# Squares of a unit taken one unit ahead, GpSimd's roots in another rhythm, block two's raw rows loaded between the contexts' loads, gates stored in scan order

## The chip, the core and the metric

The kernel runs on one core of a Trainium2 chip. The metric is the time of one execution on the device in microseconds (us), taken as the median of three runs. The engines are TensorE (PE, its weight loads PEld), VectorE (DVE), ScalarE (ACT), GpSimd (POOL) and SyncE (SP), which here only issues transfers. ACTq, POOLq and SPq are the engines' instruction queues, where transfers are issued.

## What is computed

A decoder block on 16 sequences of 256 tokens, width 256, in float32. The change touches only the first of its layers, and the preparation of the second:

```python
xn = _rmsnorm(x, norm1_w)                       # x*rsqrt(mean(x*x)+eps)*w
xc = _causal_depthwise_conv(xn, conv_w, conv_b) # 4 taps over time, then silu
q = _l2norm((xc @ wq)...); k = _l2norm((xc @ wk)...); v = (xc @ wv)...
beta = sigmoid(xc @ wb); alpha = sigmoid(xc @ wa + 4)
for each of 256 tokens, 16 sequences x 16 heads, S of 16 x 16:
    S = a * S;  pred = S^T k
    S = S + k (b * (v - pred))^T
    o = S^T q
h = x + o @ wo; then a gated MLP, layernorm
cross-attention on 120 context rows per sequence, layernorm
routed feed-forward (8 experts, top 1), layernorm
```

## The kernel before

The 256 sequence-heads stand as two halves (`h`) on 128 partitions, and the recurrence over tokens (the scan) runs on VectorE. Time is cut in two blocks of 128 tokens (`jb`), each block in 16 chunks of 8 steps, and each step updates both halves. Block one is scanned in `front_and_scan`, block two in `scan_and_post`, beside the rest of layer one and the attention.

**The front** makes the scan's input. A unit (n = 0 to 15) is 64 tokens of 4 sequences; U = 4 units make one part of 64 tokens for all sequences, and there are four parts. For a unit, SyncE loads rows (`load_rows`), ScalarE sums squares, GpSimd makes 1/rms of two columns (`inverse_rms`, L446), ScalarE (VectorE in part 0) scales the rows to `xn`, TensorE transposes, ScalarE copies to `xT`, TensorE (VectorE in part 0) convolves, ScalarE applies silu, TensorE projects, ScalarE copies q, k, v to `st` and stores them in DRAM, and copies the gates to `bst`, from where they are stored (`store_gates`, L337). A ScalarE step (`step`, L631) works on unit a, on unit b = a-1 and on unit c = a-2, in an order written out by hand. The squares of unit a stand at the head of step a, they use `xn` as scratch, and `xt`, `ss` and `rstd` have two slots. `bst` has one slot: the gate copy of a unit waits until the gate stores of the unit before have landed.

**Before a part is scanned**, `load_raw(part, h)` (L369) loads its k, q, gates and v back in scan order, for one half. This is 3 transfers of 512 KB and 8 of 8 KB on SyncE's queue. `lengths(some, h)` then makes key and query lengths, gate values and scales from them, with squares, sigmoids and square roots on ScalarE and sums and reciprocals on VectorE. For part 0 this stands before the scan. For part 1 VectorE has it woven into chunks 5 and 6 and ScalarE has it after step 2U+4 = 12; for parts 2 and 3 VectorE has it in chunks 14 and 15.

**The read-out** is GpSimd's. After each four steps it makes `outputs(c, z)`, for both halves: one multiply (L246), three folds (L252) and a last add (L254). VectorE keeps 8 states and may not overwrite one before L246 has read it (`S_read`). The same GpSimd makes the roots of units 4 to 15 between read-outs. Units 4 and 5 have theirs ahead of the first read-out and ahead of the two starting increments of `S_read` (L462), units 6 to 12 after the read-outs of chunks 0 to 3, unit 13 to 15 after those of chunks 7 and 8.

**The contexts.** When all convolutions are done, SyncE loads the attention's weights and runs a pipeline over 16 sequences: load `ct(n)`, store `kE(n-2)`, store `vP(n-2)`. `ct` has two slots. TensorE transposes context n and projects keys and values of n-1; ScalarE copies. SyncE has the four `load_raw` of parts 2 and 3 behind the whole pipeline; ScalarE has the lengths of parts 2 and 3 behind the whole pipeline.

Of the kernel before, what the change touches and what calls it, by code (L numbers as in the profile page):

```python
# [7 lines left out]
F32 = mybir.dt.float32  # L8
# [6 lines left out]
P = 128  # L15
# [7 lines left out]
NU = PARTS * U  # L23
R, Q, V, KN, KB = 8, 4, 4, 4, 2
# [7 lines left out]
CTX = 120  # L32
# [231 lines left out]
def front_and_scan(nc, sem, w, k, s, arena):  # L264
# [4 lines left out]
    with ExitStack() as ctx:  # L269
# [6 lines left out]
        xt = sb("xt", [P, 2, 2, D])  # L276
        ss, ms, rstd = (sb(n, [P, 2, 2]) for n in ("ss", "ms", "rstd"))
# [23 lines left out]
        ct, cT = sb("ct", [CTX, 2, D]), sb("cT", [P, 2, G, CTX])  # L301
# [4 lines left out]
        pa = ps("pa", [P, G, 2 * TB])  # L306
        pc = pp[:, 0, :, 0:CTX]
# [5 lines left out]
        x_in, ct_in, kv_out = ([sem(f"f_{n}{i}") for i in range(2)] for n in ("x_in", "ct_in", "kv_out"))  # L313
# [18 lines left out]
        SETUPS = 13  # L332
        TAPS = KC * G
# [3 lines left out]
        def store_gates(eng, n):  # L337

            eng.wait_ge(evac_done, n * 4 + 4)
            for i in range(2):  # L340
                for g in range(G):
                    eng.dma_start(k["gates"][i, n, g].rearrange("a q h t -> h (a q) t"),
                                  bst[32 * i + g * H // G:32 * i + (g + 1) * H // G]).then_inc(gates_out[n >= U], 16)

        @block.sync
        def _(sp):
            def load_rows(n):

                part, u, s = n // U, n % U, n % 2
                if n >= 2:  # L350
                    sp.wait_ge(xn_done, (n - 1) * 2)
# [14 lines left out]
            def load_raw(part, h):  # L366
# [5 lines left out]
                for i, name, dst in ((1, "k", x["k"]), (0, "q", x["q"]), (3, None, None), (2, "v", x["vo"])):  # L372

                    if i == 3:
                        later = part > 0
                        sp.wait_ge(gates_out[later], 64 * (units - U * later))
# [50 lines left out]
        def _(pool):  # L427
# [18 lines left out]
            def inverse_rms(a):  # L446
                if a:
                    n, slot, m = a
                    pool.wait_ge(ss_done, (n + 1) * 2)
                    nc.gpsimd.tensor_tensor(ms[:, slot], ss[:, slot], k["eps"][:, 0], ALU.add).then_inc(rstd_done, 1)  # L450
# [1584 lines left out]
```

## Time and profile before

| | |
|---|---|
| median of 3 runs | 1865.97 us (1862.27 to 1867.58) |
| the profiled execution | 1867.18 us, span 1865.5 us |
| VectorE busy | 1254.0 us, 67% |
| GpSimd busy | 1000.8 us, 54% |
| TensorE busy (matmul) | 1325.9 us, 71% |
| ScalarE busy | 849.6 us, 46% |
| first instruction of the scan | 62.01 us |
| block one's scan ends, block two's starts | about 505 us |

The page gives busy time and share for each engine, then the span in 40 slices, and last the chain that ended last. That chain shows only the end (TensorE in the routed feed-forward, from 1354 us on), so for the stages ahead of it the waits of the engine that is busy there have to be read.

### The profile page before, as it was taken

The page shows a single profiled execution, that of the slowest core. Times are in us where ns is not written, and L with a number is a line of the kernel's source. Part 1 is how long each engine was busy: PE and PEld are TensorE (multiplying, and loading weights), DVE is VectorE, ACT ScalarE, POOL GpSimd, SP SyncE. Part 2 cuts the span into 40 slices and gives each one's busy share as a digit, 9 for nine tenths or more (in the row PEclk, how much of TensorE's full clock was granted, in tenths as well). Part 3 has the DMA queues.
Part 4 walks back from the last instruction along what each step waited for, and adds up shares of the span by engine and source line. Part 5 has one row for each costly group of instructions (what it writes and reads, how often), then busy time and mean ns, then how long its engine had stood idle before and what let it go on. Part 6 is the DMA issues. An engine that isn't in the chain of part 4 may idle for free. (4 is left out here: it accounts for less than half of the span.)

```text
span 1865.5 us, 32852 instructions
## 1 busy us (share of the span) xinstructions
PE 1325.9 (71%) x9000; PEld 1151.7 (62%) x9001; DVE 1254.0 (67%) x3301; ACT 849.6 (46%) x2808; POOL 1000.8 (54%) x1234
## 2 busy tenths in 40 slices
PE   6277106850036676766765899998489999999997
PEld 4265105630025465654654778876389999999997
DVE  3798999999988999999876144454434444443442
ACT  5433213442113665667766488887322322322332
POOL 3367868987669999998866324342111122122121
PEclk9689558885568878878877999998789999999999
DMA  5344001566031010100002111133130410411200
GB/s 139 74 102 111 12 6 42 143 173 95 23 120 38 23 33 18 32 27 27 28 27 84 57 42 52 54 120 120 40 103 21 154 48 22 158 42 45 77 17 7
DMA packets 182719, 119.29 MB, mean 64 GB/s; under 512 B 124849, under 2 KB 163560, under 8 KB 182120
## 3 DMA queue, kind: packets, MB, share of 16 engines
q1 hardware_dynamic: 119848, 90.98, 17.4%
q10 hardware_dynamic: 58864, 18.71, 4.0%
q0 software_dynamic: 3920, 8.60, 1.3%
q8 instruction: 34, 0.56, 0.1%
q14 instruction: 53, 0.43, 0.1%
HBM read 83.44 MB, written 35.74 MB: 64 GB/s over the span
## 5 line engine op out<-in xcount | busy, mean ns | idle before, releaser
L246 POOL TENSOR_TENSOR wt<-wt 128x1024 f32<-128x1024 f32 x128 | 301.5, 2355 | 53.9 <-DVE wt L191 46.9
L252 POOL TENSOR_TENSOR wt<-wt 128x512 f32<-128x512 f32 (+2 forms) x384 | 307.6, 801 | 30.1
L1942 PE MATMUL e_ph<-e_g,e_w 128*128 128x128 f32 x2496 | 285.2, 275 | 0.7 <-ACT e_g L1912 0.7
L1942 PEld LDWEIGHTS e_ph<-e_g,e_w 128*128 128x128 f32 x2496 | 281.9, 192 | 0.9 <-issue 0.9
L191 DVE SCALAR_TENSOR_TENSOR wt<-wt,scan 128x256 f32<-128x256 f32 x512 | 242.0, 473 | 18.0 <-POOL wt L246 13.4
L170 DVE TENSOR_REDUCE wt<-wt 128x16 f32<-128x272 f32 x512 | 219.2, 428 | 0.1
L181 DVE TENSOR_TENSOR scan<-wt,scan 128x256 f32<-128x256 f32 x512 | 215.0, 420 | 0.3
L159 DVE TENSOR_TENSOR wt<-wt,scan 128x256 f32<-128x256 f32 x512 | 210.1, 410 | 0.9 <-PEq L269 0.5
L1420 ACT ACTIVATE wt<-p_pX,p_mx 128x120 f32<-128x120 f32 x512 | 176.4, 387 | 71.9 <-DVE p_mx L1205 70.3
L1903 ACT ACTIVATE e_g<-e_ph,wt 128x128 f32<-128x128 f32 x156 | 48.7, 363 | 304.9 <-PE e_ph L1942 304.9
L1821 POOL TENSOR_TENSOR e_ve<-e_mv,eps 128x1 f32<-128x1 f32 x39 | 7.4, 190 | 327.1 <-DVE e_mv L1877 327.1
L1554 PE MATMUL p_pm<-p_w_mix,p_oT 128*128 128x256 f32 x128 | 43.7, 500 | 160.6 <-DMA p_oT<-o 129.9
L1953 PE MATMUL e_ph<-e_xT,e_w 128*128 128x128 f32 x1248 | 148.3, 278 | 0.6 <-DVE e_xT L1858 0.6
L1953 PEld LDWEIGHTS e_ph<-e_xT,e_w 128*128 128x128 f32 x1248 | 145.0, 195 | 1.0 <-issue 1.0
L782 PE MATMUL f_pT<-ident,f_xn 128*128 128x128 f32 x64 | 15.0, 377 | 171.9 <-ACT f_xn L645 157.9
L1554 PEld LDWEIGHTS p_pm<-p_w_mix,p_oT 128*128 128x128 f32 x128 | 30.8, 252 | 170.4 <-issue 162.0
L1205 DVE TENSOR_REDUCE p_mx<-p_pX 128x8 f32<-128x960 f32 x64 | 72.9, 1150 | 75.7 <-PE p_pX L1600 75.5
L1420 ACT ACTIVATION_READ_ACCUMULATOR wt<-p_pX,p_mx 128x1 f32 x512 | 119.9, 234 | 0.0
L782 PEld LDWEIGHTS f_pT<-ident,f_xn 128*128 128x128 f32 x64 | 9.7, 188 | 177.4 <-ACT f_xn L645 162.8
L1912 ACT ACTIVATE e_g<-e_ph,wt 128x128 f32<-128x128 f32 x312 | 97.4, 363 | 42.0 <-PE e_ph L1953 41.8
L1850 DVE COPY e_w<-wt 128x4096 f32 x39 | 89.5, 2295 | 27.3 <-issue 22.2
L1566 PE MATMUL p_pX<-p_hT,p_wg 128*128 128x256 f32 x320 | 94.8, 424 | 16.7 <-ACT wt L1420 16.6
(226 smaller groups left out, 2925.0 us busy)
## 6 DMA issues: line engine op xcount, KB each, us to landing
wt<-in_L_ffn_W SPq DMA_DIRECT2D x24, 1024.0 KB
qkv<-f_st ACTq DMA_DIRECT2D x48, 256.0 KB, 2.6
p_kE<-kE SPq DMA_DIRECT2D x16, 480.0 KB, 3.7
p_vP<-vP SPq DMA_DIRECT2D x16, 480.0 KB
wt<-qkv SPq DMA_DIRECT2D x12, 512.0 KB, 6.4
e_xt<-routed ACTq DMA_DIRECT2D x39, 130.0 KB, 2.1
f_xt<-in_x SPq DMA_DIRECT2D x32, 128.0 KB, 2.8
p_oT<-o SPq DMA_DIRECT2D x16, 256.0 KB
```

The costliest lines, as they stand in the source:

```text
L159: nc.vector.tensor_tensor(s["sk"][:, h, u % V, :, 0:HD], s["S"][:, h, (u - 1) % R], s["kn"][:, h, u % KN:u % KN + 1].to_broadcast([P, HD, ...
L170: nc.vector.tensor_reduce(s["w"][:, h], s["sk"][:, h, u % V], AX, ALU.add).then_inc(s["w_done"], 1)
L181: nc.vector.tensor_tensor(s["outer"][:], s["w"][:, h].rearrange("p (v o) -> p v o", o=1).to_broadcast([P, HD, HD]), s["kn"][:, h, u % KN:u ...
L191: nc.vector.scalar_tensor_tensor(s["S"][:, h, u], s["S"][:, h, (u - 1) % R], s["gate"][:, jb, h, 2, bass.ds(c * R + u, 1)], s["outer"][:], ...
L246: nc.gpsimd.tensor_tensor(x, s["S"][:, h, z * Q:(z + 1) * Q], s["qn"][:, h, z * Q:(z + 1) * Q].rearrange("p t (o d) -> p t o d", o=1).to_b ...
L252: nc.gpsimd.tensor_tensor(x[:, :, :, 0:half], x[:, :, :, 0:half], x[:, :, :, half:2 * half], ALU.add).then_inc(s["o_fold"][h], 1)
L1420: ins = nc.scalar.activation(pr[:, x // 2, head], scores(x)[:, y // 4, y % 4], ACT.Exp, bias=mx[:, x // 2, head:head + 1], accum_out=sm[:, ...
L1566: ins = nc.tensor.matmul(gu(i)[:, which], wt[:, g, i * P:(i + 1) * P], hT[:, g], start=(g == 0), stop=(g == G - 1))
L1850: nc.vector.tensor_copy(w2[:, s].rearrange("p c f -> p (c f)"), wt[:, bass.ds(at + W2_AT, C1 * F2)]).then_inc(w2_kept, 1)
L1912: nc.scalar.activation(g1[:, c], ph1[:, c // 2, c % 2], ACT.Gelu, bias=k["bias"][:, bass.ds(at + c * NE, 1)]).then_inc(g1_done, 1)
L1942: ins = nc.tensor.matmul(ph2[:, c // 2, c % 2], w2[:, s, i, c * P:(c + 1) * P], g1[:, i], start=(i == 0), stop=(i == C1 - 1))
L1953: ins = nc.tensor.matmul(ph1[:, c // 2, c % 2], w1[:, s, g, c * P:(c + 1) * P], xT[:, g], start=(g == 0), stop=(g == G - 1))
```

## The change

- ScalarE: the squares of unit n+1 are taken in step n (`squares_of`), right after unit n is scaled, into a PSUM scratch `squared`. The unit to start with has its squares ahead of the first step. `xt`, `ss`, `ms`, `rstd` have XS = 3 slots, so `load_rows(n)` waits for unit n-3 to be scaled, not n-2.
- ScalarE's lengths of part 1 stand after step 2U+2 = 10, with the squares of unit 11 ahead of them.
- GpSimd: no root of a unit from 4 on stands before the first read-out. Units 4 to 9 have theirs after the six read-outs of chunks 0 to 2, unit 10 at the end of chunk 3, unit 11 at the end of chunk 5, units 12 to 15 after the four read-outs of chunks 7 and 8.
- Gates: the DRAM layout becomes (2, NU, a, g, q, h, t). A unit's gates are stored by 8 transfers, not 4; a half of a part is loaded by 2 transfers, not 8.
- SyncE: `load_raw(2,0)`, `(3,0)`, `(2,1)`, `(3,1)` stand after steps 2, 4, 6, 8 of the contexts' pipeline. `ct` lies in the memory of `acc`.
- VectorE's and TensorE's orders are not changed.

```diff
-                for g in range(G):
-                    eng.dma_start(k["gates"][i, n, g].rearrange("a q h t -> h (a q) t"),
+                    for a in range(2):
+                        eng.dma_start(k["gates"][i, n, a, g].rearrange("q h t -> h q t"),
...
-                if n >= 2:
-                    sp.wait_ge(xn_done, (n - 1) * 2)
+                if n >= XS:
+                    sp.wait_ge(xn_done, (n - XS + 1) * 2)
...
-                            for pair in range(U):
-                                sp.dma_start(s["gate"][32 * pair:32 * pair + 32, jb, h, 1 + y, now],
-                                             k["gates"][y, rows.start + pair // 2, :, pair % 2].rearrange("g q h t -> g (q h) t")).then_inc(gate_in[h], 16)
+                            sp.dma_start(s["gate"][:, jb, h, 1 + y, now], k["gates"][y, rows].rearrange("u a g q h t -> (u a g q h) t")).then_inc(gate_in[h], 16)
...
-            pipeline(sp, NB, 3, contexts)
-            for h in range(2):
-                for part in (2, 3):
-                    load_raw(part, h)
+            later = {2 + 2 * i: (2 + i % 2, i // 2) for i in range(4)}
+            for step in range(NB + 2):
+                contexts(*((n, n % 2, n // 2) if 0 <= n < NB else None for n in (step, step - 1, step - 2)))
+                if step in later:
+                    load_raw(*later[step])
...
-            for n in range(U, U + 2):
-                inverse_rms((n, n % 2, n // 2))
...
+            for c in range(3):
+                chunk(c, {z: (U + c * 2 + z, U + c * 2 + z) for z in range(2)})
+            chunk(3, {1: (NU - 6, NU - 6)})
+            chunk(MEASURE - 1)
+            chunk(MEASURE, {1: (NU - 5, NU - 5)})
+            chunk(MEASURE + 1)
+            chunk(MEASURE + 2, {0: (NU - 4, NU - 4), 1: (NU - 3, NU - 3)})
+            ready(1)
+            chunk(MEASURE + 3, {0: (NU - 2, NU - 2), 1: (NU - 1, NU - 1)})
...
+            def squares_of(n):
+
+                act.wait_ge(x_in[n % XS], n // XS * 32 + 32)
+                if n >= 1:
+                    act.wait_ge(rstd_done, n * 2)
+                for q in range(2):
+                    nc.scalar.activation(squared[:, q], xt[:, n % XS, q], ACT.Square, accum_out=ss[:, n % XS, q:q + 1]).then_inc(ss_done, 1)
...
+                if a is not None and a + 1 < (U if a < U else NU):
+                    squares_of(a + 1)
...
-            units(U, NU, {2 * U + 4: (*lengths(1, 0), *lengths(1, 1))})
+            units(U, NU, {2 * U + 2: (*lengths(1, 0), *lengths(1, 1))})
```

## Rows read from the trace of the kernel before

**Rows 1.** The page's busy tenths of VectorE, 40 slices of 46.6 us.
```profile
DVE  3798999999988999999876144454434444443442
```

**Rows 2.** Waits of VectorE, 0 to 120 us: us in total, times, longest.
```profile
DVE wt L191 <- POOLq L462: 4.5, 1, 4.5
```

**Rows 3.** The same view, 120 to 200 us.
```profile
DVE wt L191 <- POOL wt L246: 11.6, 6, 3.6
```

**Rows 4.** GpSimd in order of time: start, us, instruction [idle before <-releaser].
```profile
106.28 0.19 POOL L450 TENSOR_TENSOR f_ms<-f_ss,eps 128x2 f32<-128x2 f32 x1 [5.09 <-ACT f_xn L638]
107.22 0.76 POOL L230 TENSOR_TENSOR wt<-f_raw_q,f_rq 128x256 f32 x1
108.23 2.35 POOL L246 TENSOR_TENSOR wt<-wt 128x1024 f32<-128x1024 f32 x1 [0.25 <-POOL wt L230]
113.62 2.36 POOL L246 TENSOR_TENSOR wt<-wt 128x1024 f32<-128x1024 f32 x1
```

**Rows 5.** VectorE in order of time: the scales of chunks 0 and 1.
```profile
84.39 0.19 DVE L125 COPY scan<-wt 128x32 f32<-128x32 f32 x1
108.21 0.18 DVE L125 COPY scan<-wt 128x32 f32 x1
```

**Rows 6.** GpSimd in order of time: gate store of unit 1.
```profile
32.64 2.15 POOL L342 DMA_DIRECT2D gates<-f_bst  x4 [3.43 <-ACT f_bst L690]
```

**Rows 7.** ScalarE in order of time: unit 2's gate copy, and the second half's sigmoid.
```profile
38.64 0.38 ACT L690 ACTIVATE f_bst<-f_pp 48x256 f32<-48x256 f32 x1 [1.69 <-DMA gates<-f_bst]
...
57.55 0.26 ACT L703 ACTIVATE wt<-wt 128x64 f32<-128x64 f32 x1 [0.61 <-DMA wt<-gates]
```

**Rows 8.** SyncE's queue in order of time: gate loads of part 0, second half.
```profile
50.96 5.13 SPq L379 DMA_DIRECT2D wt<-gates  x8
```

**Rows 9.** GpSimd in order of time: chunk 7's first read-out.
```profile
278.45 2.34 POOL L246 TENSOR_TENSOR wt<-wt 128x1024 f32<-128x1024 f32 x1 [3.07 <-issue]
```

**Rows 10.** ScalarE in order of time: unit 15, context 15's end, key squares.
```profile
317.58 0.91 ACT L645 ACTIVATE f_xn<-f_xt,f_rstd 128x256 f32<-128x256 f32 x2 [0.61 <-POOL f_rstd L452]
...
404.03 0.45 ACT L757 ACTIVATE f_vP<-f_pp 120x128 f32<-120x128 f32 x2
420.87 1.91 ACT L712 ACTIVATE wt<-wt 128x2048 f32<-128x2048 f32 x1 [16.39 <-DMA wt<-qkv]
```

**Rows 11.** VectorE in order of time: the first sum of keys in chunk 14.
```profile
439.36 5.71 DVE L559 TENSOR_TENSOR wt<-wt 128x1024 f32<-128x1024 f32 x4
```

**Rows 12.** SyncE's queue in order of time: block two's first and last raw load.
```profile
404.92 2.67 SPq L383 DMA_DIRECT2D wt<-qkv  x2
...
446.83 0.57 SPq L383 DMA_DIRECT2D wt<-qkv  x1
```

**Rows 13.** SyncE's queue in order of time: one context load.
```profile
374.79 0.35 SPq L404 DMA_DIRECT2D f_ct<-in_ctx  x1
```

**Rows 14.** TensorE in order of time: contexts at the lower and higher clock.
```profile
359.37 0.66 PE L835 MATMUL f_pp<-ident,f_ct 120*128 120x120 f32 x2
363.72 0.43 PE L835 MATMUL f_pp<-ident,f_ct 120*128 120x120 f32 x2
...
374.17 0.42 PE L835 MATMUL f_pp<-ident,f_ct 120*128 120x120 f32 x2 [0.70 <-DMA f_ct<-in_ctx]
377.65 0.42 PE L835 MATMUL f_pp<-ident,f_ct 120*128 120x120 f32 x2 [0.68 <-DMA f_ct<-in_ctx]
```

**Rows 15.** The page's DMA issues: KB each, us to landing.
```profile
f_raw_q<-qkv SPq DMA_DIRECT2D x4, 512.0 KB, 7.2
f_vo<-qkv SPq DMA_DIRECT2D x4, 512.0 KB, 4.8
```

**Rows 16.** Stretches by engine, then TensorE's granted clock, DMA share, GB/s.
```profile
90.00:100.00 10.00, 8.89 (x31) 7.15 (x32) 10.00 (x32) 2.51 (x7) 9.23 (x9) 0.67 0.10 27
365.00:375.00 10.00, 7.95 (x47) 5.53 (x46) 10.00 (x32) 6.73 (x21) 8.83 (x12) 1.00 0.58 174
415.00:425.00 10.00, 0.00 (x0) 0.00 (x0) 10.00 (x31) 1.91 (x1) 9.17 (x8) 0.50 0.94 163
```

More of the change, by code:

```diff
@@ L275, in front_and_scan @@
         cw, cb = sb("cw", [P, G, KC]), sb("cb", [P, G])
-        xt = sb("xt", [P, 2, 2, D])
-        ss, ms, rstd = (sb(n, [P, 2, 2]) for n in ("ss", "ms", "rstd"))
+        xt = sb("xt", [P, XS, 2, D])
+        ss, ms, rstd = (sb(n, [P, XS, 2]) for n in ("ss", "ms", "rstd"))
         xn = sb("xn", [P, 2, 2, D])
@@ L312, in front_and_scan @@
         BIT, ODD, EVEN, NORM1, BIAS_K = 1, 2, 3, 4, 4 + G
-        x_in, ct_in, kv_out = ([sem(f"f_{n}{i}") for i in range(2)] for n in ("x_in", "ct_in", "kv_out"))
+        x_in = [sem(f"f_x_in{i}") for i in range(XS)]
+        ct_in, kv_out = ([sem(f"f_{n}{i}") for i in range(2)] for n in ("ct_in", "kv_out"))
         out = [sem(f"f_out_{n}") for n in "qkv"]
@@ L347, in load_rows @@
             def load_rows(n):
-                part, u, s = n // U, n % U, n % 2
-                if n >= 2:
-                    sp.wait_ge(xn_done, (n - 1) * 2)
+                part, u, s = n // U, n % U, n % XS
+                if n >= XS:
+                    sp.wait_ge(xn_done, (n - XS + 1) * 2)
                 for q in range(2):
@@ L475, in _, with chunk @@
             ready(0)
-            half = CHUNKS // 2
-            with pool.Fori(0, half - 5) as c:
+            def chunk(c, units={}):
                 for z in range(R // Q):
                     outputs(c, z)
-                    inverse_rms((c * 2 + (U + 2 + z), z, c + (U // 2 + 1)))
-            outputs(half - 5, 0)
-            inverse_rms((NU - 4, 0, NU // 2 - 2))
-            outputs(half - 5, 1)
-            with pool.Fori(half - 4, half - 1) as c:
-                for z in range(R // Q):
-                    outputs(c, z)
-            for c, z, n in ((half - 1, 0, NU - 3), (half - 1, 1, NU - 2), (half, 0, NU - 1)):
-                if c == half:
-                    ready(1)
-                outputs(c, z)
-                inverse_rms((n, n % 2, n // 2))
-            outputs(half, 1)
-            with pool.Fori(half + 1, CHUNKS) as c:
-                for z in range(R // Q):
-                    outputs(c, z)
+                    if z in units:
+                        n, slot = units[z]
+                        inverse_rms(n, slot % XS)
+            for c in range(3):
[7 more added lines that the diff above has]
+            chunk(MEASURE + 3, {0: (NU - 2, NU - 2), 1: (NU - 1, NU - 1)})
+            with pool.Fori(MEASURE + 4, CHUNKS) as c:
+                chunk(c)
         @block.vector
@@ L627, in _ @@
             act.wait_ge(set_up, SETUPS)
-            def step(a, b, c):
-                if a is not None:
-                    n, slot = a, a % 2
-                    act.wait_ge(x_in[slot], n // 2 * 32 + 32)
-                    if n >= 2:
-                        act.wait_ge(T_done, n - 1)
-                    for q in range(2):
-                        nc.scalar.activation(xn[:, slot, q], xt[:, slot, q], ACT.Square, accum_out=ss[:, slot, q:q + 1]).then_inc(ss_done, 1)
+            def squares_of(n):
[4 more added lines that the diff above has]
+                    nc.scalar.activation(squared[:, q], xt[:, n % XS, q], ACT.Square, accum_out=ss[:, n % XS, q:q + 1]).then_inc(ss_done, 1)
+            def step(a, b, c):
                 if c is not None:
@@ L724, in units @@
             def units(first, last, between):
+                squares_of(first)
                 for at in range(first, last + 2):
@@ L1977, in build @@
         "qkv": nc.dram_tensor("qkv", (3, NU, 2, G, 2, P, PT), F32, kind="Internal").ap(),
-        "gates": nc.dram_tensor("gates", (2, NU, G, 2, 2, H // G, PT), F32, kind="Internal").ap(),
+        "gates": nc.dram_tensor("gates", (2, NU, 2, G, 2, H // G, PT), F32, kind="Internal").ap(),
         "o": nc.dram_tensor("o", (JB, NB // 2, G, 2, P, TB), F32, kind="Internal").ap(),
```

34 lines of the change are left out of this document (18 added, 16 removed).

## The prediction

> **What bounds the kernel now.** I read the page's slices first. VectorE is at nine tenths and more from about 60 to 500 us, apart from two slices between 140 and 190 us at eight or just nine [rows 1]; this is block one's scan, and in it VectorE's own work or its waits set the time. All stages follow one another, and block two's scan on the same engine starts where block one's ends, so what VectorE loses or gains there reaches the end of the kernel. Second, VectorE's waits in that stage. At the scan's start it stands 4.5 us, because GpSimd gives the two starting increments only after two roots [rows 2]. Between 120 and 200 us it stands 11.6 us in six waits for the read-out's multiply [rows 3]. After that its list of waits up to 505 us is empty but for half microseconds. Of all that the change touches, only these 16.1 us are time in which VectorE stands.
>
> Third, why GpSimd is late. It waits for ScalarE's squares, 5.1 us in one case, with a read-out queued behind [rows 4]. A root costs 0.94 us (106.28 to 107.22), the queries of a chunk 1.0, and a read-out of two halves 2 x 5.39 = 10.8 (108.23 to 113.62 is one half). VectorE makes a chunk in 23.8 us [rows 5], that is 11.9 per read-out. So GpSimd has about one microsecond to spare per read-out, and a wait of 5 us for squares is not won back.
>
> **Part by part. The roots and the squares ahead.** With a root after each read-out GpSimd needs 10.8 + 0.94 + 0.6 (half of the queries, with their wait) = 12.35 us against 11.9, so it falls back 0.45 us each time, 2.7 us over six. It may fall back more than that: a read-out can start when four states are ready; the first of them is overwritten five steps later (5 x 2.98 = 14.9 us), the other half's 1.4 us after that, and the second multiply ends 7.75 us after the start [rows 4]. That leaves 8 us. The squares are there in each case, as they are taken just after the unit before is scaled, that is some 11 us ahead. So both the 11.6 and the 4.5 go: **-16.1 us**. What is late next for chunks 5 and 6 are the keys' squares of part 1 on ScalarE. Unit 10's root comes at scan start + 109 (12 us for the first four steps, six read-outs of 12.35, two of 10.8 and the root), step 10 takes some 13 us, and VectorE needs the first squares at start + 125 (five chunks and two steps): a room of 2 to 3 us. I cost it at nothing, and if it is missed, it costs up to 4.
>
> **The gate stores.** Four transfers take GpSimd 2.15 us to issue [rows 6], so eight take 4.3. For unit 0 this is paid by unit 3's root, which no longer stands ahead of it. For units 1 to 3 it adds 2.15 each, in a closed chain: ScalarE's copy of unit 2 already waits 1.69 us for unit 1's stores to land [rows 7]. The last stores land 3 x 2.15 = 6.4 us later. SyncE then issues two loads rather than eight, which took 5.13 us [rows 8], 3.9 less. The second half's sigmoid, which now waits 0.61 us for those loads [rows 7], comes 2.5 us later, and the scan starts at 64.5: **+2.5 us**, from -1 (a split store lands as early as the whole one) to +4.5 (three delays of 2.15, with only the last loads saving 2). From unit 4 on ScalarE issues eight rather than four (1.4 us more per unit) while it has time.
>
> Here a rule of the Trainium skill speaks against the change ("DMA: Bandwidth & Descriptors", Rules for kernel authors): many small transfers should be coalesced, as below 64 KB one pays mostly overhead. The row shows 0.54 us of issue per store of 8 KB, with the landings overlapped; if each further store paid the page's fixed two microseconds in turn, a unit's chain would grow by 8 us and not by 2.15, and the scan would start some 20 us later. This case's landing waits speak for the small price.
>
> **Where the front ends.** Roots now follow VectorE. Chunk 7's first read-out starts at 278.45 with GpSimd waiting [rows 9], so at 262.35 + d after the change, d being the 2.5 us above. From there four read-outs, four roots and one chunk's queries (43.2 + 3.8 + 1.3) bring unit 15's root to 310.9 + d; ScalarE takes it at 311.5 + d, and took it at 317.58 [rows 10]. ScalarE's last two gate stores cost 2.9 us more ahead of the first context. The contexts on ScalarE thus run 6.0 - 2.9 = 3.1 us earlier, plus d: without the raw loads between them they would end at 404.5 - 3.1 + d [rows 10] = 401.4 + d. The key squares of block two (1.91 us) come right behind, as their rows are long there: ready at **403.3 + d**. Now they stand until 420.87 for the rows [rows 10].
>
> **When VectorE needs them.** Its first sum of keys in chunk 14 is at 439.36 [rows 11]; it comes 16.1 us sooner: **423.3 + d**. So 20.0 us of room are left for what the raw loads do to the contexts. The cover of this edit is just that room.
>
> **The raw loads between the contexts.** Four blocks, each 3 x 512 KB, now stand ahead of a context load in SyncE's queue. A context load issued at 374.79 [rows 13] serves a transpose at 377.65, which waits for it 0.68 us [rows 14], so nothing is loaded further ahead: `ct` has two slots. What lands before it: the raw loads of one kind land 4.8 us after issue when they are alone (v), and 7.2 when one of 512 KB is 0.6 ahead (q) [rows 15], so the second adds 3.0 and the fixed part is 1.8. Three of them, the gates (0.2) and the context (0.7) give 1.8 + 9.0 + 0.9 = 11.7 us, against 377.65 - 374.79 = 2.9 now. A block delays the next context by **8.8 us**. Two further terms: the context load after it is in flight at once and saves its wait (-0.5), and TensorE has been idle for nine microseconds. After such an idle time (91 us) the stretch shows a granted clock of 0.67, near the lower level of 1.2 GHz at 0.5, against 1.00 at 2.4 GHz in the contexts [rows 16]. A context at the lower level takes 363.72 - 359.37 = 4.35 us, at the higher 3.48 [rows 14], so +0.9 for one context. Together 9.2 us a block, **36.8 us for four**. The stand of VectorE in chunk 14 is then 36.8 - 20.0 = **+16.8 us**, with d on both sides.
>
> Bounds of a block: at least SyncE's own issue, 2.67 for k and q, 0.57 for v [rows 12] and 2 x 0.64 for gates [rows 8], 4.5 us, which gives 18 < 20 and no wait. At most what a whole block takes where they stand now, (447.4 - 404.92) / 4 = 10.6 us [rows 12] at a DMA share of 0.94 [rows 16], plus 0.9: 46 us, a wait of 26. I take 9.2, as transfers on one queue have been seen to come in their order and the 4.8 and 7.2 are for the same transfers.
>
> **The sum.** -16.1 + 2.5 + 16.8 = +3.2 us on the profiled execution's 1867.18, 1870.4. That execution is 1.2 above the median of the runs, so the median goes from 1865.97 to **1869.2 us**. Everything after chunk 14 is the same code and moves with it. About 0.3% (5.6 us) is what a measurement of this kernel can tell from no change.
>
> **The rivals.**
>
> *The loads overlap (A).* If raw data and contexts share the DMA engines (contexts show a share of 0.58 [rows 16]) rather than queue, a block costs 4.5 to 5 us and VectorE never waits in chunk 14: -16.1 + 2.5 = -13.6, **1852.4**. For it: the engines have free share. Against it: the transpose waits for its context load already now, and a q behind a k lands later by a full transfer. The skill's page on DMA (same section) advises to issue early and wait late, so that the fixed cost is hidden; by that rule the loads would be free and this rival right. 28%.
>
> *TensorE's clock stays down (B), the slower side.* Its place is the contexts. With four gaps of nine microseconds, not one but most contexts run at 4.35 rather than 3.48 us: 11 more x 0.87 = 9.6, so 1869.2 + 9.6 = **1878.8**. It decides from the point where four blocks cost over 39.2 us together (2.4 beyond my sum); then the kernel is slower by over 0.3%. For it: the gap in the front brought the clock down. Against it: contexts in a row had 1.00 at once after. 17%.
>
> *The roots are not covered (C).* If unit 11's rows come late behind part 1's raw rows, step 10 and the lengths slip, half of the 11.6 comes back before chunk 7, and the contexts slip with it: 1869.2 + 5.8 = **1875.0**. The third slot and six fewer gate loads speak against it. 7%.
>
> **How the numbers follow.** My forecast has 48%, with its own range of 1863 to 1877 (a block from 7.8 to 11 us, d from -1 to 4.5). It straddles the bound of slower, at 1871.6: of the 48, 34 lie within 0.3%, 12 above and 2 below. A gives 26 to faster and 2 to same. B gives 15 to slower and 2 to same, C 5 and 2. Faster 0.28, same 0.40, slower 0.32. The range 1852 to 1879 takes in A's value and most of B.
>
> **What would show it.** The wait of 4.5 at the first state update and the waits for L246 up to chunk 5 gone (right), or still there (C). The scan's first instruction near 64.5. In the contexts four gaps of TensorE of about nine microseconds, each ended by a context load, and ScalarE's last context copy near 441. VectorE's wait for ScalarE's key squares in chunk 14, 17 us long. If the gaps are below 5 us or that wait is missing, my forecast is wrong and A right; if contexts take over 4 us each outside the gaps, B is.

## The result, and the profile after

The changed kernel takes **1873.06 us** (median of 20 runs, 1868.64 to 1877.95), the kernel before, run beside it, 1865.7 (20 runs). The ratio is **1.0037**, interval [1.0027, 1.0047]: slower by 7 us. The profiled execution took 1874.3 us, with a span of 1872.6. Forecast was 1869.2, so the changed kernel lies 3.9 us above it, inside the range, and in size just past the bound at which I had put "slower". I had given slower 32% and same 40%.

VectorE's waits come first, in the view of [rows 2, 3] (engine, what waits, for whom: us in total, times, longest). The line above the dots is all that stands between 120 and 200 us, those below it are all between 200 and 520 us:

```profile
DVE wt L559 <- ACT wt L715: 5.4, 1, 5.4
...
DVE wt L559 <- ACT wt L715: 24.7, 1, 24.7
DVE wt L160 <- DVE wt L550: 0.4, 1, 0.4
DVE scan L126 <- DVE wt L550: 0.2, 1, 0.2
```

Both old waits, the 4.5 for the increments and the 11.6 for the read-out's multiply, are gone. In their place VectorE stands twice for ScalarE's key squares: 5.4 us in chunk 5 and 24.7 us in chunk 14. VectorE in order of time (start, us, instruction, [idle before <-releaser]) shows the scan's first instruction, the two stands and the start of block two:

```profile
64.72 0.20 DVE L126 COPY scan<-wt 128x32 f32<-128x32 f32 x1 [0.23 <-DVE wt L550]
...
195.18 1.74 DVE L559 TENSOR_TENSOR wt<-wt 128x512 f32<-128x512 f32 x4 [5.38 <-ACT wt L715]
...
199.79 1.73 DVE L559 TENSOR_TENSOR wt<-wt 128x512 f32<-128x512 f32 x4
...
449.74 2.73 DVE L559 TENSOR_TENSOR wt<-wt 128x1024 f32<-128x1024 f32 x4 [24.66 <-ACT wt L715]
...
512.78 0.20 DVE L126 COPY scan<-wt 128x32 f32<-128x32 f32 x1 [0.23 <-DVE wt L550]
```

Block two starts at 512.78; in the kernel before that same instruction stands at 505.39. So the whole difference, +7.4 us, is made in block one, and it passes to the end (span +7.1). In the experiments the **start of block two** is therefore the quantity to compare between traces. A trace is one execution, though, and kernels with the same code up to the contexts don't start them at the same time: the first transpose stands at 342.2 us in one trace and at 350.0 in another (the section on the prediction comes back to this). Medians and ratios decide on the whole kernel.

TensorE's order of time in the contexts shows one block of raw loads (the first and the last row are the context behind this gap and behind the next one):

```profile
384.73 0.66 PE L839 MATMUL f_pp<-ident,f_acc 120*128 120x120 f32 x2 [7.09 <-DMA f_acc<-in_ctx]
...
389.87 0.66 PE L839 MATMUL f_pp<-ident,f_acc 120*128 120x120 f32 x2
...
401.65 0.66 PE L839 MATMUL f_pp<-ident,f_acc 120*128 120x120 f32 x2 [7.12 <-DMA f_acc<-in_ctx]
```

and SyncE's queue shows what lies ahead of the context load that ended it:

```profile
374.10 2.18 SPq L386 DMA_DIRECT2D wt<-qkv  x2
376.32 2.96 SPq L383 DMA_DIRECT2D wt<-gates  x2
379.32 0.52 SPq L386 DMA_DIRECT2D wt<-qkv  x1
379.89 1.67 SPq L407 DMA_DIRECT2D f_acc<-in_ctx  x1
```

From the first raw load to the transpose there are 384.73 - 374.10 = 10.6 us, against 2.9 for a context load alone [rows 13, 14]. The whole stage, as the group of the transposes in the tile's view (x count: duration, first to last start), after and below it before:

```profile
L839 PE MATMUL f_pp<-ident,f_acc x32: 266/407/461, 348.2 to 442.0; 120*128 120x120 f32 x32
```
```profile
L835 PE MATMUL f_pp<-ident,f_ct x32: 266/317/462, 344.0 to 398.6; 120*128 120x120 f32 x32
```

93.8 us against 54.6: 39.2 more, **9.8 a block** as compared with the kernel before. The key squares come right behind the last copy of the contexts, no longer behind their rows:

```profile
447.46 0.45 ACT L761 ACTIVATE f_vP<-f_pp 120x128 f32<-120x128 f32 x2
447.80 1.91 ACT L715 ACTIVATE wt<-wt 128x2048 f32<-128x2048 f32 x1
```

### The profile page after: what moved, and what is told of

Read it like the earlier page. It is cut to its first block and busy times, and to the rows that moved or that the text cites. A ratio compares the mean times of both kernels' runs of the same rounds, so it can differ in the third digit from the quotient of the medians.

```text
span 1872.6 us, 32656 instructions
## 1 busy us (share of the span) xinstructions
PE 1345.1 (72%) x9000; PEld 1165.9 (62%) x9001; DVE 1245.1 (66%) x3301; ACT 851.1 (45%) x2808; POOL 1007.2 (54%) x1250
## 5 line engine op out<-in xcount | busy, mean ns | idle before, releaser
L192 DVE SCALAR_TENSOR_TENSOR wt<-wt,scan 128x256 f32<-128x256 f32 x512 | 242.8, 474 | 1.8 <-POOL wt L247 1.8
L1570 PE MATMUL p_pX<-p_hT,p_wg 128*128 128x256 f32 x320 | 95.1, 425 | 17.7 <-ACT wt L1424 17.6
```

The source lines that it names most:

```text
L192: nc.vector.scalar_tensor_tensor(s["S"][:, h, u], s["S"][:, h, (u - 1) % R], s["gate"][:, jb, h, 2, bass.ds(c * R + u, 1)], s["outer"][:], ...
L1570: ins = nc.tensor.matmul(gu(i)[:, which], wt[:, g, i * P:(i + 1) * P], hT[:, g], start=(g == 0), stop=(g == G - 1))
```

## The experiments

Two parts of the change can be undone each by itself: where the raw loads stand, and how the gates are stored. The first four runs make the table of these, the others take single costs out.

**The raw loads behind the contexts** (the rest as changed).

```diff
-            later = {2 + 2 * i: (2 + i % 2, i // 2) for i in range(4)}
-            for step in range(NB + 2):
-                contexts(...)
-                if step in later:
-                    load_raw(*later[step])
+            pipeline(sp, NB, 3, contexts)
+            for h in range(2):
+                for part in (2, 3):
+                    load_raw(part, h)
```

> The changed kernel with the four raw loads of block two back behind the contexts' pipeline; nothing else differs. My theory (each raw block ahead of a context load holds the contexts back by 9.8 us, 39 us in all, and VectorE waits 24.7 us in chunk 14 for that): the contexts take 54 us again from the first transpose to the last instead of 93.7, ScalarE is done with them near 408, the key rows land some 14 us behind that, near 423, VectorE needs the squares near 425, so its wait in chunk 14 is 0 to 3 us. The kernel gains 22 to 25 us on the changed one less some 3 us of sums that run slower beside a busy GpSimd: 1851 us, 0.992 of before. Rival (the contexts are slow from TensorE's clock or from their late start, not from the loads' place): the contexts still take over 75 us and the time stays within 8 us of the changed kernel's 1873.

Measured: 1854.68 us, ratio 0.9942 [0.9929, 0.9956]. The key squares are taken at 424.54 after 13.2 us of waiting for the rows, and VectorE, which needs them then, waits 0.5:

```profile
424.54 1.91 ACT L714 ACTIVATE wt<-wt 128x2048 f32<-128x2048 f32 x1 [13.21 <-DMA wt<-qkv]
```

Where the rows are waited for the squares are in time; where the rows are loaded early the squares are late. Against the changed kernel the loads' place costs 1.0037 - 0.9942 = 0.0095, **17.7 us**. That is the step on which the forecast hung, and it had 16.8. The two numbers are not the same thing, however. The forecast's 16.8 was the stand in chunk 14; that stand is 24.2 us longer with the loads between the contexts (24.7 against 0.5), and part of it is given back by faster sums, so that block two starts 20.8 us later (512.78 against 491.94). The kernel is 3.7 us slower than I expected of it, and the contexts are not as short as I expected:

```profile
L838 PE MATMUL f_pp<-ident,f_acc x32: 266/317/462, 346.0 to 405.4; 120*128 120x120 f32 x32
```

59.4 us, where I had expected 54. So of the 39.2 us by which this stage grew, the loads' place makes 34.4, that is **8.6 a block** and not 9.8. The other 4.8 are there without any load between the contexts.

**Only the raw loads between the contexts** (the kernel before, with the lines above put in).

> The kernel before, with only the raw loads of block two put between the contexts, after steps 2, 4, 6 and 8. My theory: the contexts end 39 us later, at 443.7, the key squares are ready at 445.6 and VectorE needs them at 439.4; it waits 6 us, of which its sums give 3 back as they meet no busy GpSimd: 3 us slower than before, 1869, ratio 1.002. Rival (the loads overlap with the contexts and the loss of the changed kernel comes from its other parts): no wait in chunk 14, ratio 1.000 and the contexts end before 425.

Measured: 1877.93 us, ratio 1.0067 [1.0053, 1.0081], more than twice what I expected. The sign was right, the size was not: the kernel before loads gates by eight transfers, and between contexts these eight cost much. SyncE's queue in this run, and its transposes:

```profile
348.54 2.57 SPq L383 DMA_DIRECT2D wt<-qkv  x1
351.15 5.91 SPq L379 DMA_DIRECT2D wt<-gates  x8
```
```profile
L836 PE MATMUL f_pp<-ident,f_ct x32: 266/324/462, 340.7 to 442.6; 120*128 120x120 f32 x32
```

5.91 us of issue, and a stage of 101.9 us, 11.8 a block rather than 9.8. VectorE stands 14.0 us in chunk 14 and keeps the 4.5 at the scan's start and 9.0 of the 11.6 for the read-out.

**The gates as before** (the rest as changed, raw loads between the contexts): four stores for a unit, eight loads for a half.

```diff
-                    for a in range(2):
-                        eng.dma_start(k["gates"][i, n, a, g]..., bst[..., 2 * a:2 * a + 2])...
+                    eng.dma_start(k["gates"][i, n, g].rearrange("a q h t -> h (a q) t"), bst[...])...
```

> The changed kernel with the old gate layout: four stores for a unit, eight loads for a half of a part. My theory: the scan starts at 62.0 again instead of 64.7, and in the front's steady part ScalarE's round of a unit falls from 15 or 16 us by the 1.4 us of the four issues, so that the last unit is scaled some 7 us earlier and the contexts start and end 7 us earlier; VectorE's wait in chunk 14 ends with them: 1866 us, ratio 1.000. Rival (the stores are hidden and the late start of the contexts comes from TensorE alone): the rounds stay within 0.5 us, the time falls by at most 2.7 us, 1870 or more.

Measured: 1869.8 us, ratio 1.0023 [1.0013, 1.0033]. The scan starts at 63.24, not 64.72, chunk 5's stand is gone, chunk 14's is 22.0, and the contexts take 101.1 us (334.2 to 435.3). I had expected 1866 us and a front that ends 7 us earlier. It ends 13 us earlier than in the changed kernel's trace (unit 15 is scaled at 309.40 and not at 322.34), and the contexts, now with eight gate loads in each block, eat more than half of that.

**Both undone**: raw loads behind the contexts and gates as before. What is left of the change are the squares one unit ahead, the roots and the third slot.

> The changed kernel with both undone: raw loads behind the contexts and the old gate layout. What remains is the squares one unit ahead, the third slot of rows, the roots' rhythm and the lengths of part 1 after step 10. My theory: the waits of 4.5 and 11.6 us stay away, the scan starts at 62.0, the wait in chunk 5 is below 5.4 us as the units run faster, none in chunk 14: 16 to 20 us faster than before, 1846 to 1850, ratio 0.990 to 0.992. Rival (the gain was eaten by something in the roots' rhythm itself): over 1858.

Measured: **1849.15 us, ratio 0.991 [0.9896, 0.9924]**, the fastest kernel of all, 0.9% faster than the kernel before and 1.3% faster than the changed one, and inside the range that I had expected. Its contexts take 50.7 us (333.6 to 384.3), at a granted clock of 1.00 up to 390 us. VectorE has no wait over half a microsecond from 120 us to the start of block two, which comes at 486.60.

| ratio to the kernel before | gates as before | gates changed | gates' price |
|---|---|---|---|
| raw loads behind the contexts | 0.9910 | 0.9942 | 0.0032, 6.0 us |
| raw loads between the contexts | 1.0023 | 1.0037 | 0.0014, 2.6 us |
| price of the loads' place | 0.0113, 21.1 us | 0.0095, 17.7 us | |

That the gates cost time behind the contexts is clear. Between them it is 0.0014, with an interval of 0.0010 to either side on each of the two ratios, so that it is hardly clear of nothing; and whether the gates cost less there than behind is not shown: by the starts of block two they cost 6.7 us between the contexts and 5.3 behind them, the other way round. The loads' place costs 17 us or more in either column.

**Part 1's rows first** (raw loads of block two behind the contexts, gates changed, and `load_raw(1, h)` one unit later in SyncE's queue, so that unit 11's rows go ahead). In the changed kernel ScalarE waits for those rows, and key squares come at 194.09, in order of time:

```profile
185.94 0.39 ACT L635 ACTIVATE f_squared<-f_xt 128x256 f32<-128x256 f32 x1 [8.42 <-DMA f_xt<-in_x]
...
194.09 1.06 ACT L715 ACTIVATE wt<-f_raw_k 128x1024 f32<-128x1024 f32 x1 [2.87 <-issue]
```
```diff
-                if n in (2 * U + 1, 2 * U + 2):
-                    load_raw(1, n - 2 * U - 1)
+                if n in (2 * U + 2, 2 * U + 3):
+                    load_raw(1, n - 2 * U - 2)
```

> The changed kernel with the raw loads behind the contexts and, further, the loads of part 1's raw rows one unit later in SyncE's queue, so that unit 11's rows are ahead of them. In the changed kernel ScalarE waits 8.4 us for those rows in step 10, and VectorE 5.4 us in chunk 5 for the key squares behind (6.0 in the variant with the loads behind the contexts alone, which took 1854.7). My theory: ScalarE's wait of 8 us goes, silu still waits for TensorE, the key squares come 4 us earlier, VectorE waits 1 to 2 us in chunk 5: 1850.5 us, ratio 0.992. Rival (ScalarE is late by its own round of 16 us a unit, not by the rows): the wait stays at 5 to 6 us and the time at 1854.7.

Measured: 1855.28 us, ratio 0.9931 [0.9912, 0.9951]. The squares stand at 186.66 and chunk 5's wait is gone, as expected, but block two starts only 3.2 us sooner (488.77 against 491.94) and the ratio can't be told from 0.9942. The cause of the 5.4 us, rows that come late, is confirmed; that it is worth 4 us to the whole kernel is not.

**The same, with the gates as before.** Here VectorE has no stand in chunk 5 to be cured.

> The changed kernel with the raw loads of block two behind the contexts, the gate stores and loads as before, and part 1's raw loads one unit later in SyncE's queue, so that unit 11's rows come ahead of them. Roots and squares alone (the first two of these) took 1849.2, ratio 0.991, with no wait of VectorE in chunks 5 and 14. Theory: where VectorE does not stand, moving the rows buys nothing, 1849 to 1850, ratio 0.991. Rival: the 8.9 us that ScalarE waits for unit 11's rows still costs VectorE something through later units, then 1845 to 1847, ratio 0.989.

Measured: 1850.52 us, ratio 0.9923 [0.9901, 0.9945]; block two starts at 486.71, against 486.60. ScalarE's wait of 8.9 us for the rows is gone, and nothing came of it: idle time of an engine for which nobody waits.

**Four slots for the contexts**: everything as changed, but the context loads have four slots (in the memory of `xn`, idle by then) and go out two further ahead of the raw loads.

```diff
-                    if since(n, 2):
-                        sp.wait_ge(cT_done, n - 1)
-                    sp.dma_start(ct[:, slot], ...).then_inc(ct_in[slot], 16)
+                    if since(n, 4):
+                        sp.wait_ge(cT_done, n - 3)
+                    sp.dma_start(ct[:, n % 4], ...).then_inc(ct_in[n % 4], 16)
...
+            for n in range(2):
+                contexts(ahead(n), None, None)
...
+                contexts(ahead(step + 2), None, ahead(step - 2))
```

> The changed kernel with four slots for the contexts instead of two, so that the loads of contexts n+1 and n+2 are ahead of each raw block in SyncE's queue. My theory (a block's price is the waiting of one context load behind 1.5 MB in the same queue, as nothing is loaded further ahead): two contexts can be worked on during a block, and what remains is the DMA engines' own time, 9.3 us for the block and some 2.1 for each context, 13.5 us a pair against 16.7 now and 7 without blocks. The contexts take 26 us more than without blocks and not 39, the wait in chunk 14 falls from 24.7 to 12 us: 1860 us, ratio 0.997. Rival (it is only the depth of the slots): pairs of about 10 us, wait of 2 us or none, 1851. Rival (the block's issue on SyncE holds it): pairs stay at 16 or more, 1872.

Measured: 1857.81 us, ratio 0.9947 [0.9927, 0.9967]. The raw loads stay where the change has put them, and yet 0.0090 of the 0.0095 is back:

```profile
L842 PE MATMUL f_pp<-ident,f_xn x32: 266/321/462, 342.2 to 410.2; 120*128 120x120 f32 x32
```
```profile
416.07 1.91 ACT L718 ACTIVATE wt<-wt 128x2048 f32<-128x2048 f32 x1
```

The contexts take 68.0 us, 3.4 a block where it was 9.8 (2.2 where it was 8.6, against the 59.4 of the same kernel without loads between), and the squares come at 416.07. VectorE doesn't stand in chunk 14. So a block is dear because no context is loaded ahead of it. I had thought that a good part of it was transfer time that no depth can hide. By the contexts and by the missing wait the rival, that depth alone decides, was nearer; the time, 1857.81, lies between its 1851 and my 1860.

**The queries' load alone moved behind the contexts** (k, gates and v stay between them), to price one transfer of 512 KB.

```diff
-                    load_raw(*later[step])
+                    load_raw(*later[step], "k3v")
+            for h in range(2):
+                for part in (2, 3):
+                    load_raw(part, h, "q")
```

> The changed kernel with the q part of each raw block (512 KB of 1.5 MB) moved behind the contexts. My theory (bytes in the queue ahead of the context load): each gap of TensorE shrinks by 3.0 us, from 7.1 to about 4.1, a pair takes 13.7 us, ScalarE ends the contexts 12 us earlier, the wait for the key squares falls from 24.7 to 12.7 us; the q rows land some 8 us after the last context, so VectorE waits about 2 us for the q squares: 1863 us, ratio 0.9985. Rival (a fixed price for each interruption): the gaps stay near 7 us and the time at 1873.

Measured: 1866.91 us, ratio 0.9994 [0.9976, 1.0012], between my 1863 and the rival's 1873. The profiled execution, 1872.79, is the slowest of the twelve. The contexts take 80.6 us (350.0 to 430.6), 13.2 less than 93.8, so **3.3 us for each 512 KB**, and a pair takes 13.7 us as I had said. But it doesn't come about as I had said:

```profile
381.53 0.66 PE L843 MATMUL f_pp<-ident,f_acc 120*128 120x120 f32 x2 [6.50 <-DMA f_acc<-in_ctx]
...
385.94 0.43 PE L843 MATMUL f_pp<-ident,f_acc 120*128 120x120 f32 x2
...
395.21 0.66 PE L843 MATMUL f_pp<-ident,f_acc 120*128 120x120 f32 x2 [6.47 <-DMA f_acc<-in_ctx]
```

The gap has shrunk from 7.1 to 6.5 us only, where I had expected 4.1 and the rival some 7. The two contexts behind it take 395.21 - 6.47 - 381.53 = 7.2 us, where they took 9.8 in the changed kernel, and the granted clock over them is 0.76 where it was 0.54. From the block's first raw load to the transpose, 8.3 us pass (386.89 to 395.21) and not 10.6, so 2.3 us is what the transfer itself adds in the queue. The rest of the 3.3 comes from the contexts, which ran at a higher clock. VectorE stands 14.2 us in chunk 14, in two waits.

**TensorE kept busy in the gaps**: 28 matmuls that nothing reads ahead of contexts 3, 5, 7 and 9. The results of the kernel don't depend on them.

```diff
-            pipeline(pe, NB, 2, keys_values)
+            for step in range(NB + 1):
+                if step in (3, 5, 7, 9):
+                    for _ in range(28):
+                        nc.tensor.matmul(pT[...], ident[:], xc[...], start=True, stop=True)
+                keys_values(...)
```

> The changed kernel with 28 matmuls of 128x128x256 into a bank that nobody reads, on TensorE ahead of contexts 3, 5, 7 and 9, in the gaps that the raw blocks leave. It separates the clock's part of a block from the queue's. Clock theory: the context after a gap takes 3.5 us and not 5.14, a pair 15.1 us and not 16.7, so the contexts end 6.5 us earlier and the kernel takes 1867 us. Rival (the context after a gap is slow because its stores and the next load go through SyncE late, whatever the clock): pairs stay at 16.7, 1873.

Measured: 1877.52 us, ratio 1.0062 [1.0041, 1.0082], 10 us above what I had expected. This run was badly sized: the matmuls took 12.2 us, longer than the gap they were to fill. But the context behind them shows the clock's part. TensorE in order of time:

```profile
365.55 0.37 PE L839 MATMUL f_pp<-ident,f_acc 120*128 120x120 f32 x2
...
368.22 0.42 PE L839 MATMUL f_pp<-ident,f_acc 120*128 120x120 f32 x2
```

A context takes 368.22 - 365.55 = 2.67 us, where in the changed kernel it takes 389.87 - 384.73 = 5.14.

**The same with 16 matmuls**, which take some 7 us and fit.

> The changed kernel with 16 matmuls of 128 columns that nothing reads put on TensorE ahead of contexts 3, 5, 7 and 9. The 28 of the run before took 10.96 us, 0.39 each, so 16 take about 6.3 us and fit into the gap of 8.7 to 6.9 us that stood before these contexts. If the low clock after a gap is a part of a block's price, as my theory has it, the context after a gap takes about 2.7 us rather than 5.14, a pair about 14.3 rather than 16.7, the contexts about 9.8 us less than 93.7, VectorE's stand in chunk 14 about 15 rather than 24.7, and the kernel comes to 1863 to 1866. The rival, that all of a block's price is the loads' landing: the gap grows by as much as the context after it shrinks, pairs stay at 16.7 and the time at 1873 (ratio 1.0037).

```profile
383.70 0.43 PE L839 MATMUL f_pp<-ident,f_acc 120*128 120x120 f32 x2 [0.87 <-DMA f_acc<-in_ctx]
...
386.44 0.43 PE L839 MATMUL f_pp<-ident,f_acc 120*128 120x120 f32 x2
...
398.15 0.42 PE L839 MATMUL f_pp<-ident,f_acc 120*128 120x120 f32 x2 [1.67 <-DMA f_acc<-in_ctx]
```

Measured: 1869.34 us, ratio 1.0017 [0.9998, 1.0035]. A context behind a gap takes 2.74 us, a pair 14.45 (383.70 to 398.15) and VectorE stands 14.9 us in chunk 14, as expected. The contexts take 87.1 us in all (346.7 to 433.8), 6.7 less and not 9.8 less, and the time is above the expected 1863 to 1866. The rival has a part in it: without its two contexts (2.74 and 2.87 us) the pair leaves 8.8 us, where the gap was 7.1, so part of what the contexts gain is lost again in front of the next load. Block two starts 8.1 us sooner (504.64). Of this the profiled execution keeps 5.1 and the ratio 0.0020, 3.7 us, with an interval that overlaps that of the changed kernel. So by these two traces the low clock makes 1.7 us of a block's 9.8; that the whole kernel gains by the filling is not clear of noise, and what became of the other 3 us behind block one is open.

## Why the prediction came out as it did

**-16.1 for the two waits: right.** Both are gone from the trace, and the kernel in which only squares, roots and slots are changed is 16.8 us faster (0.0090 of 1865.4). That this is so near to 16.1 is in part luck: in its trace block two starts 18.8 us sooner, of which 2.7 are faster sums in chunks 5 and 6 (10.4 us against 13.1), while the scan starts 0.9 later.

**Rival C, at 7%: its condition came true.** Unit 11's rows came late behind part 1's raw rows, step 10 and the lengths slipped, and VectorE lost 5.4 us before chunk 7, where the rival had 5.8 (half of the 11.6). Only its sign was wrong: the time came back as a wait for the key squares and not for L246. The third slot and six fewer gate loads, which were to speak against it, did not prevent it.

**Chunk 5, costed at nothing, at most 4: it came to 5.4.** In the six traces of kernels that are the same up to there it is 2.6, 3.2, 5.4, 5.7, 6.0 and 6.0 us, so the bound of 4 was too tight, if not in each execution. The step looked at unit 10's root, and the root was not what was late. With a whole `load_raw` of part 1 in SyncE's queue ahead of them (issued from 171.69 to 180.6), unit 11's rows arrive late and hold ScalarE 8.4 us before the key squares. With the gates as before ScalarE still waits 8.9 us there, and VectorE doesn't notice; only together with the longer rounds of eight gate stores (below) does it bite. Loading those rows first, or going back to four gate stores, removes it, each by itself.

**+2.5 for the gate stores up to the scan's start: right in the sum** (64.72, +2.7; forecast 64.5), in part by luck. With the gates as before the scan starts at 62.88 to 63.24 in three traces, so about one of the 2.7 us comes from the rest of the change, which the forecast had at nothing, and the gates make 1.5 to 1.8. The chain of stores looks as costed, with 0.55 us of issue for each: GpSimd, and ScalarE's copy behind the landing, in order of time:

```profile
32.78 4.44 POOL L347 DMA_DIRECT2D gates<-f_bst  x8 [2.74 <-ACT f_bst L693]
```
```profile
41.48 0.38 ACT L693 ACTIVATE f_bst<-f_pp 48x256 f32<-48x256 f32 x1 [4.54 <-DMA gates<-f_bst]
```

Against the Trainium skill's rule on many small transfers ("DMA: Bandwidth & Descriptors", Rules for kernel authors), which the prediction had weighed, these rows say: twice as many stores of half the size cost their issue and not a fixed latency each, so the scan came 2.7 us later and not 20.

**Where the front ends: this step failed.** The prediction let GpSimd's roots set the pace (unit 15 scaled at 314.0; its own terms add up to 313.75) and said that ScalarE issues eight gate stores "while it has time". It has none. ScalarE in order of time, one round of the changed kernel:

```profile
291.16 0.91 ACT L646 ACTIVATE f_xn<-f_xt,f_rstd 128x256 f32<-128x256 f32 x2 [0.52 <-ACT f_st L681]
...
299.24 0.84 ACT L656 ACTIVATE f_xc<-f_pa,f_cb 128x256 f32<-128x256 f32 x2 [6.37 <-PE f_pa L799]
...
303.43 2.74 ACTq L347 DMA_DIRECT2D gates<-f_bst  x8
306.28 0.60 ACT L681 ACTIVATE f_st<-f_pp 128x512 f32<-128x512 f32 x1 [2.88 <-PE f_pp L817]
...
307.40 0.91 ACT L646 ACTIVATE f_xn<-f_xt,f_rstd 128x256 f32<-128x256 f32 x2 [0.52 <-ACT f_st L681]
```

and of the kernel with the gates as before and the raw loads behind the contexts:

```profile
297.13 0.91 ACT L646 ACTIVATE f_xn<-f_xt,f_rstd 128x256 f32<-128x256 f32 x2 [0.52 <-ACT f_st L681]
...
302.24 0.84 ACT L656 ACTIVATE f_xc<-f_pa,f_cb 128x256 f32<-128x256 f32 x2 [3.40 <-PE f_pa L799]
...
306.43 1.35 ACTq L346 DMA_DIRECT2D gates<-f_bst  x4
...
309.01 0.91 ACT L646 ACTIVATE f_xn<-f_xt,f_rstd 128x256 f32<-128x256 f32 x2 [0.52 <-ACT f_st L681]
```

A scaling waits for a root in neither (0.52 us behind ScalarE's own copy, where before it was 0.61 for GpSimd [rows 10]). The round is a ring of ScalarE and TensorE: 16.2 us with eight stores, 11.9 with four. The issue is only 1.4 of these 4.3; the wait for the convolution grows from 3.4 to 6.4. The stretches of both rounds, changed kernel first (columns as in [rows 16]), show TensorE's clock:

```profile
291.20:307.40 16.20, 13.45 (x48) 10.43 (x48) 16.20 (x51) 5.41 (x16) 15.26 (x17) 0.79 0.20 51
```
```profile
297.13:309.01 11.88, 10.48 (x48) 8.20 (x48) 11.88 (x37) 5.45 (x16) 10.91 (x14) 1.00 0.27 71
```

The same 48 matmuls keep TensorE busy for 13.45 us at a granted clock of 0.79 and for 10.48 at 1.00. Which part is the stores' and which the clock's can be read from another trace. The kernel with four slots for the contexts has the changed kernel's code up to the contexts, eight gate stores among it, and in its trace the clock was 1.00 in this round:

```profile
293.64 0.84 ACT L659 ACTIVATE f_xc<-f_pa,f_cb 128x256 f32<-128x256 f32 x2 [3.40 <-PE f_pa L802]
...
297.83 2.75 ACTq L347 DMA_DIRECT2D gates<-f_bst  x8
```
```profile
288.53:301.80 13.27, 10.48 (x48) 8.21 (x48) 13.27 (x42) 5.45 (x16) 12.43 (x14) 1.00 0.24 62
```

Its round takes 13.27 us, and its wait for the convolution is 3.40 again. So eight stores cost a round the 1.4 us of their issue, and the other 3.0 of the changed kernel's trace are the clock's. The clock is not low in every execution with eight stores. In the last two rounds, up to unit 15, it was 1.00 throughout in three of the seven traces that there are, and down to 0.79 or 0.88 in at least one of the two rounds in the other four. In the three traces with four stores it was 1.00 in both rounds. That the longer round is what lets the clock fall is thus likely but not shown, and why it falls in one execution and not in another is open.

So unit 15 is scaled at 322.34 in the changed kernel's trace, 8.3 us later than forecast, and the first transpose comes at 348.2 rather than 343.4 (344.0 before, 3.1 earlier, plus 2.5), 4.8 later. In the traces in which the clock was 1.00 (four slots, and 28 matmuls), unit 15 is scaled at 315.06 and 315.55 and the first transpose comes at 342.2 and 342.5. There the forecast's number is nearly met, but not by its mechanism: no scaling waits for a root, the ring sets the pace. With four stores unit 15 is scaled at 309.0 to 309.4, earlier than the 311.5 that the forecast's roots would allow without the 2.5 us of gate stores.

**A block of raw loads, 9.2: measured 9.8, the mechanism right, two terms missized.** (Against the same kernel with the loads behind the contexts it is 8.6; the forecast compared with the kernel before.) The gap was 7.1 us (the first of the four 8.7) instead of 8.3, and the low clock cost more than the 0.9 I had allowed: the two contexts behind a gap take 5.14 + 4.66 us (401.65 - 7.12 - 389.87) instead of twice 3.48. The 0.9 came from a misreading of [rows 14]. The 3.48 at the higher level contain 0.68 of waiting for a load; without it a context takes 2.7, as the kernels with filled gaps show. And the 4.35 were not all at the lower level, as the granted clock from 359.37 to 363.72 was 0.61. Further on the clock is at the lower level, 0.50 (the same view, 415 to 425 us):

```profile
415.00:425.00 10.00, 6.67 (x24) 5.14 (x24) 10.00 (x31) 2.67 (x8) 8.18 (x10) 0.50 0.51 142
435.00:445.00 10.00, 8.57 (x50) 6.18 (x50) 0.00 (x0) 6.83 (x22) 0.00 (x0) 1.00 0.59 172
```

This is rival B's mechanism: eight of the sixteen contexts run slow, at over 4 us each, and the clock is back at 1.00 once the gaps have ended. By the forecast's own measure (3.48 a context) it cost 4 x 2.8 = 11.4 us, where the forecast had 3.6 and B 13.2. B's total, 1878.8, was not reached: the gaps were shorter than forecast, and faster sums took time back (see the sum). Rival A, that the loads overlap, is refuted by these gaps; the four slots, with 3.4 us a block and no wait in chunk 14, show that it would have been right had contexts been loaded ahead. The rule of the Trainium skill that spoke for A ("DMA: Bandwidth & Descriptors", Rules for kernel authors: issue early, wait late) held for the raw loads themselves, whose rows nobody waited for any more. It did not hold for the context loads, which the raw loads made late.

**When VectorE needs the squares: 423.3 + d = 425.8 forecast, 425.08 measured, and right by two errors.** VectorE stood 5.4 us in chunk 5 which I hadn't counted, and it saved 5.5 us that I hadn't counted either: its sums of squares in chunks 5 and 6 went from 13.1 to 7.6 us of busy time (below).

**The stand: 16.8 forecast, 24.7 measured.** The squares are ready at 447.80 + 1.91 = 449.7 against 403.3 + 2.5 + 36.8 = 442.6: 7.1 later, of which 4.8 is the front and 2.4 the blocks. The 4.8 is this trace's; by the traces with a clock of 1.00 in the front it would be nothing.

**The sum.** -16.1 + 2.7 + 5.4 - 5.5 + 24.7 - 3.0 = +8.2 by the terms that the traces name (-5.5 and -3.0 are faster sums, explained in the last section; the -3.0 is the sum in chunk 14, 5.71 us before [rows 11] and 2.73 after), +7.4 by the start of block two; 0.8 stay without a name. Forecast +3.2. The forecast erred by 7.9 in the stand and 5.4 in chunk 5, and 8.5 of faster sums took most of this back. That the time came within 4 us of the forecast is therefore in good part luck.

## What to carry to other kernels

Moving big loads ahead in a queue isn't free because the engines behind have slack: price what stands *behind* them in that queue, and first give that a deeper prefetch (here two more slots turned 9.8 us a block into 3.4). Before "engine X has time" is written down, close the ring in which X works: if its round already equals its own work plus its partners', every microsecond of issue is paid in each round (1.4 us here), and if TensorE's clock is low in that round, that comes on top (3.0 here). A part of a change that removes a wait on the engine that sets the time is worth testing alone: here it was worth 0.9%, and two companions that looked harmless spent more than that.

## What the runs showed of the hardware that I had not expected

**VectorE's sums are faster while GpSimd stands.** The same four instructions of L559, 512 columns first, took 4.77 and 4.16 us in chunk 5 of the kernel before, beside GpSimd at work, and 1.74 and 1.73 in the changed kernel (rows above), where GpSimd had nothing to do from 194.97 to 204.27:

```profile
203.75 4.77 DVE L559 TENSOR_TENSOR wt<-wt 128x512 f32<-128x512 f32 x4
...
211.41 4.16 DVE L559 TENSOR_TENSOR wt<-wt 128x512 f32<-128x512 f32 x4
```
```profile
194.21 0.76 POOL L231 TENSOR_TENSOR wt<-f_raw_q,f_rq 128x256 f32<-128x256 f32 x1
204.27 2.35 POOL L247 TENSOR_TENSOR wt<-wt 128x1024 f32<-128x1024 f32 x1 [9.31 <-issue]
```

So a stand of VectorE for ScalarE is partly repaid, as GpSimd runs out of work meanwhile: 3.0 us in chunk 14. In chunks 5 and 6 it is 5.5, but 2.7 of these come without a stand too (in the kernel with both parts undone), so only the rest can be a repayment. The Trainium skill has the mechanism ("SBUF — State Buffer", SBUF: two separate sides): VectorE, for an instruction with two inputs in SBUF, and GpSimd, for one that reads SBUF, need the same pair of ports, and the one that starts second waits for the whole instruction of the other. The trace agrees in size: what a sum loses, 3.0 and 2.4 us, is about one multiply of GpSimd (2.35). I had not applied it. The steps of the scan, which have one input in `scan` (a PSUM tile), don't show it: L191 takes 473 ns on the mean beside a busy GpSimd in the kernel before, and its line in the changed kernel, L192, takes 0.47 us at 197.84 too, where GpSimd has nothing to do.

**Gate loads of 8 KB between big ones**: eight of them took SyncE 5.91 us, and a block 2.0 us more than with two loads of 32 KB (11.8 against 9.8), from runs that differ in other parts too; with only the gates different it was 101.1 against 93.8 us of contexts, 1.8 a block. The clock differs between these traces as well. Against the same kernels with the loads behind the contexts (50.7 and 59.4 us) a block costs 12.6 us with eight gate loads and 8.6 with two.
